# Adding up and copying the flag of missed rows earlier in each step of a sparse-attention kernel

## The reference

```python
dots = jnp.einsum('bhij,hk->bkij', dots, pre_proj)
dots = jnp.where(causal[None, None], neg, dots)
top = lax.top_k(dots, SPARSE_TOPK)[0]      # SPARSE_TOPK = 64
vk = top[..., -1:]                          # the 64th largest of each row
dots = jnp.where(dots < vk, neg, dots)
attn = jax.nn.softmax(dots, axis=-1)
attn = jnp.einsum('bhij,hk->bkij', attn, post_proj)
```

## Time and profile before

| | us |
|---|---|
| median of 3 runs | 4384.43 (4381.63 to 4387.21) |
| the profiled execution, its own time | 4384.25 |
| its span from the first to the last instruction | 4382.4 |
| PE busy | 3044.8 (69%) |
| DVE busy | 3024.4 (69%) |
| ACT busy | 2805.6 (64%) |
| POOL busy | 1981.4 (45%) |
| mean granted PE clock | 0.808 of full speed |

### The profile page before, as it was taken

One profiled execution on the slowest core, in us unless ns is written; L12 is line 12 of the kernel. 1 busy time (PEld: TensorE's weight loads), 2 busy tenths in 40 slices (PEclk: granted clock), 3 DMA queues, 4 the chain that ended last, 5 costly groups with the idle time before them and its releaser, 6 DMA issues. The chain is left out here.

```text
span 4382.4 us, 71286 instructions
## 1 busy us (share of the span) xinstructions
PE 3044.8 (69%) x13751; PEld 2004.1 (46%) x13751; DVE 3024.4 (69%) x14030; ACT 2805.6 (64%) x7482; POOL 1981.4 (45%) x3688
## 2 busy tenths in 40 slices
PE   8677766777766777667676766776666777677764
PEld 4344444444444444445444434444444444444443
DVE  4676777677677766776776777767677677667764
ACT  1766666666656666666666656666666666666662
POOL 3344444444444444444444444443544444454443
PEclk9888878877888787888788878778788878878776
DMA  1000000000000000000000000000000000000000
GB/s 34 6 2 1 4 6 4 7 4 6 1 4 7 4 6 2 4 7 4 6 4 7 2 4 6 4 7 1 4 6 4 7 2 4 6 4 7 1 6 3
DMA packets 31417, 22.76 MB, mean 5 GB/s; under 512 B 3201, under 2 KB 30338, under 8 KB 30722
## 3 DMA queue, kind: packets, MB, share of 16 engines
q1 hardware_dynamic: 30722, 16.03, 1.3%
HBM read 11.83 MB, written 4.19 MB: 4 GB/s over the span
## 5 line engine op out<-in xcount | busy, mean ns | idle before, releaser
L875 ACT ACTIVATE signs<-scores,state 128x528 int8<-128x528 f32 (+2 forms) x2304 | 1445.2, 627 | 1347.9 <-DVE state L1106 1298.2
L1293 POOL TENSOR_SCALAR probs<-probs,rinv 128x528 f32<-128x528 f32 (+3 forms) x1024 | 538.9, 545 | 2231.6 <-DVE rinv L1135 2229.7
L1034 DVE MAX8 state<-work 128x8 f32<-128x528 f32 (+3 forms) x1024 | 472.0, 506 | 780.2 <-ACT flags L807 769.8
L1301 POOL TENSOR_TENSOR work<-scores,work 128x528 f32<-128x528 f32 (+3 forms) x1024 | 887.0, 899 | 13.8 <-DVE work L1020 13.8
L719 PE MATMUL s_bank<-xn,gT 128*128 128x512 f32 (+3 forms) x2048 | 857.1, 544 | 6.7 <-ACT gT L807 5.5
L743 PE MATMUL t_bank<-ident,probs 128*128 128x128 f32 x2560 | 588.8, 393 | 317.1 <-POOL probs L1293 192.4
L605 PE MATMUL misc<-b_all,xn 128*128 128x512 f32 x512 | 387.2, 848 | 603.2 <-ACT u_all L807 468.9
L743 PEld LDWEIGHTS t_bank<-ident,probs 128*128 128x128 f32 x2560 | 461.3, 205 | 596.2 <-issue 336.0
L730 PEld LDWEIGHTS y_bank<-u_all,probsT 128*128 128x128 f32 x5120 | 641.0, 200 | 138.3 <-issue 127.4
L730 PE MATMUL y_bank<-u_all,probsT 128*128 128x128 f32 x5120 | 646.3, 284 | 10.2 <-ACT probsT L886 10.2
L1130 DVE SCALAR_TENSOR_TENSOR probs<-scores,kth,expo 128x528 f32<-128x528 f32 (+3 forms) x1024 | 521.6, 565 | 62.1 <-issue 58.5
(11 more groups left out here) (152 smaller groups left out, 3331.4 us busy)
## 6 DMA issues: line engine op xcount, KB each, us to landing
xwork<-in_L_attn_x_dram SPq DMA_DIRECT2D x17, 256.0 KB, 2.8
xres<-in_L_attn_x_dram SPq DMA_DIRECT2D x16, 256.0 KB, 2.9
out_dram<-ybuf SPq DMA_DIRECT2D x16, 256.0 KB, 2.4
u_all<-in_L_attn_Wq_dram SPq DMA_DIRECT2D x1, 512.0 KB, 3.9
u_all<-in_L_attn_Wk_dram SPq DMA_DIRECT2D x1, 512.0 KB, 4.7
u_all<-in_L_attn_Wv_dram SPq DMA_DIRECT2D x1, 512.0 KB, 5.3
u_all<-in_L_attn_Wo_dram SPq DMA_DIRECT2D x1, 512.0 KB
expo<-in_L_ffn_w_gate_dram SPq DMA_DIRECT2D x1, 192.0 KB, 4.8
```

Source lines behind the costliest of these rows:

```text
L875: nc.scalar.activation(signs[:, k, 0:ROW[t]], row(scores, ring(head_of(s, k + 1), RING), t), ACT.Sign, bias=guesses(s % STATES, k, GUESSES ...
L1034: v.max(candidates(past)[:, t, 1:9], work[:, s % 2, AT[t]:AT[t] + ROW[t]]).then_inc(select_step, 1)
L1293: nc.gpsimd.tensor_scalar(prb, prb, rinv[:, slot_p, t:t + 1], 1.0, ALU.mult, ALU.mult).then_inc(scaled, 1)
L1301: nc.gpsimd.tensor_tensor(wrk, row(scores, slot_k, t), wrk, ALU.subtract).then_inc(hidden, 1)
```

## The change

The flag keeps its instructions and moves within the step. In the list of uses of the two `misc` banks it now stands before the second extra product. PE makes it right behind G, ahead of `weigh`. ACT copies it right behind `gT`, ahead of `count(0)`. Two helper functions that relied on the flag being the last use of a batch now compute its place. DVE's and POOL's programs stay as they are.

```diff
@@ misc_order
         if makes_g(kind, s):
             uses.append(("G", s + 1))
-        uses.append(extra(kind, s, 1))
         if flagged(kind, s):
             uses.append(("FLAG", s))
+        uses.append(extra(kind, s, 1))
@@ new, and used by g_index and flag_index for s == 0
+def from_last(kind, b, use):
+    back = {len(USES[k]) - PLACE[k][use] for k in {"mid": ("first", "mid"), "last": ("mid",), "drain": ("last",)}[kind]}
+    assert len(back) == 1
+    return misc_index(kind, b, USES[kind][0]) - back.pop()
@@ PE, step(s)
                     make_extra(kind, b, par, s, 0)
                     if makes_g(kind, s):
                         product_g(kind, b, par, par if s < H - 1 else 1 - par, s + 1)
+                    if flagged(kind, s):
+                        pe.wait_ge(bad_ready, g - LAG_E + 1)
+                        share(kind, b, ("FLAG", s))
+                        nc.tensor.matmul(misc[misc_place(kind, par, ("FLAG", s))][0:1, 0:T + 1], lhsT=onesP[:, 0:1],
+                                         rhs=missed[:, :], start=True, stop=True).then_inc(misc_full, 1)
...
                         weigh(head_of(s, LAG_V), g - LAG_V)
                     make_extra(kind, b, par, s, 1)
                     if lagged(kind, s, LAG_P):
                         for q in range(3):
                             turn(head_of(s, LAG_P), g - LAG_P, q)
-                    if flagged(kind, s):
...
@@ ACT, step(s)
                         take(kind, b, par, ("G", s + 1), gT[(s + 1) % 2][:, :])
+                    if flagged(kind, s):
+                        at_least(act, probs_ready, 4 * (g - LAG_E))
+                        take(kind, b, par, ("FLAG", s), flags[:, :], misc[misc_place(kind, par, ("FLAG", s))][0:1, 0:T + 1])
                     count(0)
                     take_extra(1)
...
                     take_turned(2)
-                    if flagged(kind, s):
...
```

More of the change, by code:

```diff
@@ L219, in g_index @@
         return misc_index("pro", 0, ("G", H))
-    return misc_index(kind, b, USES[kind][0]) - 2
+    return from_last(kind, b, ("G", H))
 def flag_index(kind, b, s):
@@ L227, in flag_index @@
         return misc_index(kind, b, ("FLAG", s - 1))
-    return misc_index(kind, b, USES[kind][0]) - 1
+    return from_last(kind, b, ("FLAG", H - 1))
 def ln_index(kind, b, what):
@@ L919, in step @@
                     take_turned(2)
-                    if flagged(kind, s):
-                        at_least(act, probs_ready, 4 * (g - LAG_E))
-                        take(kind, b, par, ("FLAG", s), flags[:, :], misc[misc_place(kind, par, ("FLAG", s))][0:1, 0:T + 1])
                 for s in range(H):
```

## The result

The changed kernel takes 4003.55 us (median of 4 runs, 4002.62 to 4005.65), against 4384.02 us for the kernel before in the same comparison. The ratio is 0.9132 with a 95% interval of 0.9117 to 0.9148. The forecast was 4034 us, with a range of 3930 to 4165 us, and 3985 to 4110 us for the likeliest case by itself. The gain is 380 us where 350 were forecast.

A forecast was written before the change was run, and what follows sets the result against it. ACT and DVE waiting for each other through the flag was taken to bound the kernel, 15.58 us a step. Saving 22.2 us a batch over 15.75 batches gives 350 us: 4384.25 - 350 = 4034 us, range 3930 to 4165 us.

The forecast's parts named there:

- the likeliest case: The forecast itself: ACT's ordinary step at 13.6 us, 4034 us in all, own range 3985 to 4110; chance 0.67.
- The loop through the flag: ACT's step to the flag's copy, then DVE to the next moved guesses: 11.06 + 0.73 + 3.59 + 0.20 = 15.58 us.
- The load: Loading the flag into DVE's register at its third MAX8: may show for 0 to 0.73 us.
- The next floor: POOL's offset and DVE's own work arrive together, giving 13.1 us per ordinary step, 14.65 in steps 11 to 13.
- rival one: POOL and DVE bind everywhere, ACT keeps up: 26.7 us a batch, 420 us, giving 3964 us; chance 0.14.
- `weigh` behind the flag: On PE, weigh delays the second extra product; ACT stands 1.6 us, its step growing from 11.06 to 12.65 us.
- The clock: PE's clock falls in about half of the steps, costing about 1.0 us a step on average; bounds 0 and 3.5.
- The sum over a batch: Gains of 9.8 us in steps 3 to 7, 10.9 in 10 to 15, about 1.5 elsewhere: 22.2 us a batch.
- ACT's wait for the guesses: ACT's wait until DVE has moved the guesses (L1106) falls from 1298 to some 400 to 600 us.
- rival two: Low PE clock in most steps, ACT's ordinary step 15.0 us, about 10.5 us gained a batch: 4219 us; chance 0.10.
- Three: Low PE clock in every step for all of the way, ACT's step 16.1 us: 4415 us; chance 0.06.
- Four: No change: another wait takes its place, DVE waiting at L1130 for ACT's exponentials; 4384 us, chance 0.03.

The follow-up runs named there:

- experiment 2: Changed kernel, but ACT copies the flag behind count(0) instead of ahead of it, 2.1 us later: 4006.66 us, ratio 0.9132.
- experiment 7: Kernel before's order for weigh and second extra product, flag's product behind them on PE, ACT copying right behind that product (7.95 us into its step): 3939.58 us.
- experiment 8: Kernel before with PE's flag product behind weigh and second extra product, ACT copying behind its second probability copy, 10.40 us into its step: 4209.29 us.
- experiment 1: Changed kernel, but PE runs weigh ahead of the flag's product instead of behind it: 3939.46 us, ratio 0.8982.
- experiment 4: Changed kernel with weigh ahead of the flag's product on PE and POOL's offset of the next step made early: 3650.70 us, ratio 0.8324.
- experiment 6: Changed kernel with 24 unread transposes on PE between G and the flag's product: 3972.41 us, ratio 0.9064.

## Why the prediction was right

**The loop through the flag.** Right. The period was the sum of ACT's step, the load and DVE's way to the moved guesses. With the flag early the wait fell to nothing (forecast: under 40 us). Experiments 2, 7 and 8 show the other half of the step: a copy at 7.5 or 8.0 us costs no time, one at 10.4 us does. The load, which was allowed 0 to 0.73 us, shows for nothing.

**The next floor.** Right. POOL's `offset` and DVE's own way were to give 13.1 us in an ordinary step. In experiment 1, in which only this loop is left, the medians of seven of the eight ordinary steps are 12.96 to 13.08 us, the eighth is 13.36, and the time is 3939 us, where rival one's sum was 3964. The two ways did not arrive together: DVE stands 0.98 us for `offset` in the step above, and with `offset` early (experiment 4) ordinary steps take 12.2 to 12.6 us. So POOL's `offset` is the floor.

**`weigh` behind the flag.** Right in kind, and right in the sum by two errors that cancel. ACT's stall for the second extra product was put at 1.6 us at full clock and 1.0 more for the clock. In the step above it is 2.40 us, and ACT's 124 waits for the values average 2.7 us (339.7 / 124). But at full clock it is only 0.8 us (the median of the 69 waits for the values in experiment 6 whose `weigh` ran at full clock): the flag's product and the first weights took 0.12 us and not 0.55, and ACT wants the product 2.80 us after its first copy and not 2.52. The clock adds the rest, nearly 2 us. The stall costs 64 us in all by experiment 1.

**The clock.** Here the forecast was wrong. It had PE's idle ahead of the flag shorter than the 2.85 us of the earlier trace rows and took the clock to fall in about half of the steps. The idle is 908.8 / 256 = 3.55 us on average, with a median of 2.57 us. In 148 steps it is shorter than 2.85 us as forecast, and in 111 of these the lower level holds for more than half of `weigh` all the same; of all 256 steps it does in 215. That one idle of 2.85 us had passed without a fall did not carry over to others of that length. The median of `weigh`'s matmuls is 421 ns, their time at the lower level, and their mean rose from 284 to 378 ns. Still the mean clock of the whole run rose from 0.808 to 0.846, as forecast. The rule of the Trainium skill, page "TensorE: Matmul & The Clock Gate", section "HAM oscillation — how this bites in real kernels", that bursts after waits can start cold, fits this kernel better than I took it to: 124 of the 256 `weigh` begin at the lower level, and in most of the others the clock falls on the way. What it could not give is the time, since the greater part of the stall lies under the floor of `offset`.

**The sum over a batch.** From one batch's first to its last moved guesses (L1106 before, L1113 after), and the two stretches of the earlier trace rows:

```profile
L1113 DVE TENSOR_TENSOR state<-state,move x17: 171/171/172, 2004.1 to 2242.1; 128x12 f32<-128x12 f32 x17
...
L1113 DVE TENSOR_TENSOR state<-state,move x6: 171/171/171, 1991.0 to 2058.7; 128x12 f32<-128x12 f32 x6
...
L1113 DVE TENSOR_TENSOR state<-state,move x7: 171/171/172, 2094.6 to 2177.7; 128x12 f32<-128x12 f32 x7
```

| stretch | before | forecast | measured | gain forecast | gain, mean of 16 batches |
|---|---|---|---|---|---|
| steps 3 to 7 | 76.8 | 67.0 | 67.7 | 9.8 | 9.6 |
| steps 10 to 15 | 96.7 | 85.8 | 83.1 | 10.9 | 12.2 |
| the other five | 87.4 | 85.9 | 87.2 | 1.5 | 1.9 |
| the batch | 260.9 | 238.7 | 238.0 | 22.2 | 23.7 |

Before, forecast and measured are for the one batch of the rows; the last column is worked out from all starts of L1106 and L1113.

The mis-sized terms are these. Steps 10, 14 and 15 were charged with ACT's longer step of 13.6 to 14.1 us and take 13.4, 13.0 and 13.4 us. ACT's own step is 13.7 us and more there, as forecast, but ACT may lag behind DVE by some us before DVE waits for it, and catches up in the steps with layernorms: it waits for the guesses in only 127 of 256 steps. The four steps behind the layernorms kept their periods within 0.5 us, as forecast, and step 1 gained 2.1 us instead of 1.5; in the one batch of the rows the five together gained only 0.2 us. Step 0 is 0.2 us longer and step 2 0.4 us. In experiment 1 they are not, and there DVE waits for ACT's exponentials once (1.7 us), here in 38 cases (44.5 us at L1137). That this wait is the cause was not tested by itself.

The remaining 30 us of the gain beyond the forecast are about 23 us by the gain of a batch (23.7 us and not 22.2) and 7 by the number of batches: the L1113 run from 116.8 to 3930.1 us in 257 periods of 14.8 us (L1106 ran from 114.5 to 4307.6, 16.3 us each), which is 16.06 batches, and the forecast took 15.75.

**ACT's wait for the guesses** was forecast at 400 to 600 us and is 308. Beside it stand the 616.5 us of ACT's waits for PE; in experiment 1, which takes most of these away, the wait for the guesses is 807.5 us.

**The rivals.** One is what happens with `weigh` moved out of the way (3939 us). Of two the condition came and the time did not: the clock is low in most steps. But rival two gave ACT's step 15.0 us, and its medians are 13.0 to 14.8 us in the steps ahead of ordinary ones that have a second extra product. ACT catches up in the layernorm steps, and so the ordinary steps take 13.0 to 13.8 us. That the forecast's time held with a clock so much worse than forecast is partly luck, by the two errors above. Three did not come either. Four did not come: the exponentials hold DVE for 44.5 us in all.

## What to carry to other kernels

When two engines wait for each other in turn, move the small result that closes the loop to any place at which it is early enough, and work out that point: here 4.52 us ahead of the next floor. Earlier than this brings nothing, and it can cost: put the product behind the large work of its engine and not ahead of it. After the fix look at once for the next wait; here it was a small POOL instruction at the end of a long step, and moving it brought 232 us. Count on a part of such a wait coming back elsewhere: 195 of its 514 us came back as longer instructions of DVE.

## What the runs showed of the hardware

Small two-input instructions of DVE get longer beside work of POOL. In experiment 4 a SCALAR_TENSOR_TENSOR over 128x24 numbers took up to 1136 ns, where 183 ns is its usual time, and the POOL passes beside it are 1040 to 1300 ns long:

```profile
2008.13 1.13 DVE L1095 SCALAR_TENSOR_TENSOR between<-product,between 128x24 f32<-128x24 f32 x1
```

```profile
2007.93 1.30 POOL L1229 TENSOR_TENSOR ybuf<-xres,ybuf 128x512 f32<-128x512 f32 x1
```

The DVE instruction starts 0.20 us behind POOL's and ends at 2009.26, 0.03 us after it. It is so in each of the 21 cases in which L1095 is long: it ends about 40 ns behind POOL's pass. With the passes cut to 4 columns the longest fell to 231 ns. The Trainium skill, page "SBUF — State Buffer", section "SBUF: two separate sides", says that DVE and GpSimd share a pair of ports under an exclusive lock held for a whole instruction, for a DVE instruction with two SBUF inputs against a GpSimd one that reads SBUF. These ends agree with that. In the kernels with the late `offset`, DVE waited for POOL's last instruction of the step ahead of these small instructions, which kept the two apart: in experiment 1 no instruction of POOL runs beside L1095, and it never takes over 185 ns. So a part of the time won by overlap is given back: DVE is busy for 191 us more in experiment 4 than in experiment 1.

The granted clock can fall after an idle stretch is over, and then meets the first work behind it: in the step of the changed kernel shown first, at about 2010.8 us (the mean of that stretch is 0.90), 0.7 us after PE had started again. The length of the idle alone does not tell it: 2.56 us were followed by a fall here, and 2.85 us were not in the earlier trace rows. Filling the idle with 24 transposes a step that nobody reads won 31 us.
